# The orders of all five engine queues of a four-layer attention chain are rewritten, and its first five loads are dealt anew to two DMA-issuing queues

## Chip, cores and metric

One NeuronCore of a Trainium2 chip runs the kernel. The metric is the device time of one execution in microseconds (us), over three runs of the kernel before: 165.75, 165.82 and 166.11, median 165.82. A profiled execution of the same kernel is a run of its own and has its own time.

## What is computed

The input x is 8 images of 16 x 16 tokens with 128 channels, in float32. Four layers follow each other. Reduced to what matters (pieces of the reference; projections, biases and the second branch of layer 3 are left out):

```
# layer 0: attention with pooled keys and values
attn = softmax(theta(x) @ maxpool2x2(phi(x)).T)          # 256 x 64 an image
x = x + (attn @ maxpool2x2(g(x)) @ w_o + b_o) * sigma
# layer 1: group norm, attention with one head of 128 channels
x = x + softmax(q(gn(x)) @ k(gn(x)).T / sqrt(128)) @ v(gn(x)) @ wo + bo   # 256 x 256
# layer 2: group norm, attention with 8 heads of 16 channels
x = x + concat(softmax(q_h @ k_h.T / 4) @ v_h) @ w_out + b_out            # 8 x 256 x 256
# layer 3: Hartley transform over channels and width, block MLP, soft threshold, inverse
y = o2k + o2n
y = sign(y) * relu(abs(y) - 0.01)
x = x + dht2d(y) / (W * C)
```

Nothing passes from one image to another.

## The kernel before

The whole problem stays in the core's memory: the inputs are loaded once (x as tokens, `xin`; x with channels on the partitions, `x0T`; one table of weights, `tab`, in five column groups), and each image's result is stored once. All arithmetic is float32, for which each product on TensorE takes two passes, so a product shows as two MATMUL records.

Nothing schedules the work at run time. `build` holds five blocks, one for each engine queue: `sp` (SyncE, DMA issues alone), `pool` (GpSimd), `pe` (TensorE), `act` (ScalarE) and `dve` (VectorE). In each, small functions are defined that first wait for a semaphore of the step whose result they need and then issue that step for image i; behind them stands a list of calls, written out by hand, that is the order of that engine's queue. An engine works through its list strictly in that order. Extra pairs such as `("theta", 6)` in a call are added waits: on TensorE they hold a step until a PSUM bank's earlier content has been read, since the second argument of a TensorE call is the bank (0 to 7) that it writes.

The names used below, one call an image unless stated, with the line of the instruction in the profile:

- layer 0: `proj0` (TensorE L525), `pool0` (VectorE L1091), `pg_out` (GpSimd L407) and `phi_out` (L402), `theta` (ScalarE L870, two instructions), `s0` (TensorE L541), `nmax0_out` (VectorE L1097), `exp0` (ScalarE L888), `p0t` (TensorE L548, a transposition), `p0c` (ScalarE L895), `gwm` (TensorE L533), `gw` (ScalarE L881), `o0` (TensorE L556), `inv0_out` and `x1_out` (VectorE L1104, L1111), `x1b_out` (GpSimd L344);
- group norm before layers 1 and 2 (the second argument): `x1t`/`x2t` (TensorE L564/L628), `moments`, `mean` (VectorE L1121, L1126), `mean_square` (GpSimd L420), `gm1`/`gm2` (TensorE L571/L637), `variance`, `variance_eps` (VectorE L1133, L1139), `inverse_deviation` (GpSimd L359), `normalised` (VectorE L1148);
- layer 1: `qk1`, `v1m`, `s1` (TensorE L581, L590, L599), `q1`, `v1` (ScalarE L900, L907), `nmax1_out` (VectorE L1156), `score_shift` (GpSimd L429, two instructions), `exp1` (ScalarE L914), `p1t` (TensorE L609), `p1c` (ScalarE L921), `o1` (TensorE L619), `inv1_out`, `x2_out` (VectorE L1163, L1170), `x2b_out` (GpSimd L351);
- layer 2, heads in two sets g = 0 and 1: `qk2`, `v2m` (TensorE L647/L648, L655), `qkE`, `qkO`, `va` (ScalarE L928, L935, L941), `sm` (scores for the maxima, TensorE L671), `nmax2_out` (VectorE L1181, two halves a set), `nt` (TensorE L681), `nc_out` (ScalarE L948), `spread` (SyncE L287: a DMA of 8 KB that lays the maxima beside the queries), `st` (scores again, transposed and shifted, TensorE L692), `exp2` (ScalarE L954, two halves a set), `pv` (TensorE L703), `oc` (ScalarE L960), `ot` (TensorE L714), `oinv_out`, `on_out` (VectorE L1188, L1194), `ont` (TensorE L722), `onc` (ScalarE L965), `o2` (TensorE L730), `x3_out` (VectorE L1202);
- layer 3: `zm`, `am`, `ym`, `v3`, `om` (TensorE L744, L753/L755, L765/L766, L773, L782), `zc`, `odd_out`, `o1k_out`, `o1n_out`, `yh`, `s3_out` (ScalarE L970, L976, L982, L989, L998, L1003), `wrap`, `z_sum`, `z_difference` (GpSimd L365, L370, L413), `a_out`, `yn`, `xo` (VectorE L1211/L1212, L1219, L1227), `store` (SyncE L292).

Steps on weights alone (`fold_biases`, `fold_values`, `fold_biases2`, `fold_out2`, `fold_mlp` on TensorE; `scaled1`, `scaled2`, `bias_wide`, `bias_wide2`, `mlp_sums` on GpSimd; `values_scores`, `fold1_out` on ScalarE; `halves`, `mlp_folded` and others on VectorE) are strewn in among the first images. `keep_clock(n, b)` (TensorE L464) issues n bf16 products of zeros into bank b whose result nobody reads.

The five groups of the weight table are called tab0 (73.5 KB: the bias columns and `w0`, needed by the first product), tab1 (128 KB), tab2 (640 KB), tab3 (384 KB) and tab4 (708 KB). Two queues issue loads: SyncE and, for the first two of its own, ScalarE.

Of the kernel before, what the change touches and what calls it, by code (L numbers as in the profile page):

```python
# [126 lines left out]
def build(nc, x, xT, xT_rest, weights, out):  # L127


    with ExitStack() as ctx:  # L130
# [180 lines left out]
        def _(pool):  # L311
# [121 lines left out]
            pg_out(0); pg_out(1); phi_out(0); pg_out(2); phi_out(1); pg_out(3, ("gw_ps", 1), ("phi", 1)); phi_out(2)  # L433
            scaled1(0); phi_out(3, ("s0", 1)); scaled1(1); bias_wide(); scaled1(2); mean_square(0, 1); pg_out(4)
            scaled2(0); x1b_out(0); x1b_out(1); bias_wide2(); inverse_deviation(0, 1); mean_square(1, 1); x1b_out(2)
            scaled2(1); mlp_sums(); inverse_deviation(1, 1); mean_square(2, 1); score_shift(0); pg_out(5); x1b_out(3)
            pg_out(6); inverse_deviation(2, 1); scaled2(2); phi_out(4); phi_out(5); phi_out(6); pg_out(7, ("phi", 5))
            phi_out(7, ("s0", 5)); score_shift(1); x2b_out(0); mean_square(0, 2); mean_square(3, 1); score_shift(2)
            inverse_deviation(0, 2); x1b_out(4); mean_square(4, 1); inverse_deviation(3, 1); x2b_out(1); x2b_out(2)
            mean_square(1, 2); score_shift(3); mean_square(2, 2); inverse_deviation(1, 2); x1b_out(5)  # L440
            inverse_deviation(4, 1); inverse_deviation(2, 2); x1b_out(6); x2b_out(3); score_shift(4)
            mean_square(5, 1); mean_square(6, 1); mean_square(3, 2); inverse_deviation(5, 1); inverse_deviation(6, 1)
            x1b_out(7); inverse_deviation(3, 2); x2b_out(4); score_shift(5); score_shift(6); mean_square(4, 2)
            mean_square(7, 1); inverse_deviation(4, 2); inverse_deviation(7, 1); x2b_out(5); x2b_out(6); wrap(0)
            z_sum(0); z_difference(0); score_shift(7); mean_square(5, 2); mean_square(6, 2); x2b_out(7)
            inverse_deviation(5, 2); inverse_deviation(6, 2); wrap(1); mean_square(7, 2); z_difference(1); z_sum(1)
            inverse_deviation(7, 2); wrap(2); z_sum(2); z_difference(2); wrap(3); z_sum(3); z_difference(3); wrap(4)
# [4 lines left out]
        def _(pe):
# [339 lines left out]
            s0(3, 7, ("vo_rd", 1)); proj0(5, 6, ("gw", 4)); x1t(2, 0); proj0(6, 5, ("gw", 5))
            proj0(7, 2, ("b2_rd", 1)); fold_out2(3); qk1(0, 1); gm1(1); p0t(3, 3, ("o2_rd", 1)); v1m(0, 7); s1(0, 1)
            o0(3, 3); keep_clock(6, 6, ("theta", 6), ("v1", 1)); fold_mlp(6, 7); gm1(2); qk1(1, 3, ("x1", 4))
            gwm(5, 4); p1t(0, 1); s1(1, 3); v1m(1, 4, ("gw", 6)); s0(4, 1, ("p1T", 1))
            o1(0, 6, ("fold1_rd", 1), ("c_rd", 1)); qk1(2, 0); s0(5, 7); v1m(2, 2, ("theta", 8)); x1t(3, 4)
# [483 lines left out]
```

## Time and profile before

| | before |
|---|---|
| device time, three runs | 165.75, 165.82, 166.11 us (median 165.82) |
| profiled execution: its own time | 164.78 us |
| profiled execution: span of the core | 162.9 us |
| TensorE matmuls busy | 154.6 us |
| VectorE, ScalarE, GpSimd busy | 103.2, 107.1, 53.2 us |
| instructions | 3840 |

The span runs from the first to the last recorded instruction; the profiled execution's own time is 1.88 us longer and holds what lies around it, and the median of the unprofiled runs is 1.04 us above that time. TensorE's busy share is that of matmul records, which overlap their neighbours by a pipeline depth, so a busy TensorE may still be one that waits in small pieces.

### The profile page before, as it was taken

To read this page: it belongs to the slowest core of one execution; us is meant where nothing else is said; L and a number is where in the kernel's file an instruction comes from. 1 tells how busy PE (TensorE), PEld (TensorE's weight loads), DVE (VectorE), ACT (ScalarE), POOL (GpSimd) and SP (SyncE) were. 2 spreads that over 40 slices of the span, in tenths; PEclk is the share of its full clock that TensorE was granted. 3 is DMA by queue.
4 is the path that set the end of the run, shared out by engine and by line. 5 is a ranking of instruction groups with operands and counts; after the bars stand their busy time and mean duration, and the time that the engine had idled before them with its cause. 6 is when DMAs were issued, how large, how long until landed. Compare 5 with 4: busy or idle time off the path is not lost.

```text
span 162.9 us, 3840 instructions
## 1 busy us (share of the span) xinstructions
PE 154.6 (95%) x1461; PEld 118.7 (73%) x1461; DVE 103.2 (63%) x257; ACT 107.1 (66%) x245; POOL 53.2 (33%) x128
## 2 busy tenths in 40 slices
PE   5999999999999999999999999999999899999992
PEld 3899789877867677886576865777588576568892
DVE  0447977979789648665997664984397554015453
ACT  3577469854855685858366765838856768885770
POOL 6474988653722541530201153002002000016300
PEclk9999999999999999999999999999999999999999
DMA  5995000000000000000000000000001000100003
GB/s 146 252 395 209 0 6 4 0 4 0 0 0 8 0 0 4 4 0 6 0 4 4 4 32 4 0 10 0 0 4 36 32 8 4 36 0 0 0 4 129
DMA packets 3233, 5.50 MB, mean 34 GB/s; under 512 B 400, under 2 KB 2320, under 8 KB 3216
## 3 DMA queue, kind: packets, MB, share of 16 engines
q1 hardware_dynamic: 2928, 5.00, 9.1%
q8 instruction: 12, 0.20, 0.5%
q10 hardware_dynamic: 288, 0.26, 0.5%
q14 instruction: 5, 0.04, 0.1%
HBM read 4.08 MB, written 1.05 MB: 31 GB/s over the span
## 4 chain that ended last, share of the span: by engine, by line
PE 83%; ACT 5%; DVE 4%; POOL 2%; issue 2%; DMA 2%; SPq 0%; DVEq 0%; POOLq 0%
PE psum L692 9%; PE psum L703 9%; PE psum L671 9%; PE psum L619 5%; PE psum L599 5%; ACT pT L954 4%; PE psum L647 3%; PE psum L730 3%; PE psum L714 3%; PE psum L765 2%; PE psum L744 2%; PE psum L773 2%; PE psum L590 2%; DVE nmax L1181 2%; PE psum L609 2%; PE psum L766 2%
## 5 line engine op out<-in xcount | busy, mean ns | idle before, releaser
L1181 DVE TENSOR_REDUCE nmax<-psum 128x4 f32<-128x1024 f32 x32 | 38.1, 1218 | 10.2 <-PE psum L671 10.2
L954 ACT ACTIVATE pT<-psum 128x1024 f32<-128x1024 f32 x32 | 31.2, 1020 | 12.6 <-PE psum L692 12.6
L365 POOL COPY zE<-zE 128x17 f32<-128x17 f32 x8 | 1.6, 200 | 51.4 <-ACT zE L970 51.4
L692 PE MATMUL psum<-qk 32*128 32x256 f32 (+1 forms) x256 | 18.2, 399 | 0.1
L671 PE MATMUL psum<-qk 16*128 16x256 f32 (+1 forms) x256 | 18.1, 396 | 0.0
L703 PE MATMUL psum<-pT,vaug_all 128*32 128x256 f32 x256 | 17.1, 385 | 0.3 <-ACT pT L954 0.3
L692 PEld LDWEIGHTS psum<-qk 32*128 32x128 f32 (+1 forms) x256 | 11.6, 184 | 4.5 <-issue 1.8
L671 PEld LDWEIGHTS psum<-qk 16*128 16x128 f32 (+1 forms) x256 | 11.7, 184 | 4.0 <-DVE nmax L1181 1.2
L429 POOL TENSOR_SCALAR nb<-nmax,e 128x1 f32<-128x1 f32 x16 | 5.8, 372 | 19.3 <-DVE nmax L1156 11.1
L703 PEld LDWEIGHTS psum<-pT,vaug_all 128*32 128x32 f32 x256 | 6.8, 109 | 6.4 <-issue 2.5
L1148 DVE TENSOR_SCALAR xn<-psum,rstd 128x256 f32<-128x256 f32 x16 | 8.5, 540 | 2.6 <-POOL rstd L359 2.6
L359 POOL TENSOR_TENSOR rstd<-vare,half 128x1 f32<-128x1 f32 x16 | 8.7, 555 | 3.3 <-DVE vare L1139 3.1
L619 PEld LDWEIGHTS psum<-v_all,p1T 128*128 128x128 f32 x64 | 7.8, 191 | 1.6 <-issue 1.6
L351 POOL TENSOR_TENSOR x0T<-x,b_out 128x256 f32<-128x256 f32 x8 | 5.8, 728 | 9.4 <-DVE x L1170 9.4
L619 PE MATMUL psum<-v_all,p1T 128*128 128x129 f32 x64 | 8.9, 281 | 0.0
L599 PE MATMUL psum<-xn,t1T 128*128 128x256 f32 x32 | 8.6, 392 | 0.0
L914 ACT ACTIVATE p<-psum,nb 128x256 f32<-128x256 f32 x16 | 6.7, 473 | 2.9 <-POOL nb L429 2.7
L960 ACT COPY oT<-psum 128x256 f32<-128x256 f32 x16 | 5.9, 371 | 3.8 <-PE psum L703 3.6
L420 POOL TENSOR_SCALAR mv<-mv 128x1 f32<-128x1 f32 x16 | 5.4, 343 | 9.1 <-DVE mv L1126 9.0
L464 PE MATMUL psum<-busy 128*128 128x256 bf16 x35 | 6.7, 313 | 1.4 <-DVE busy L1030 1.0
L870 ACT ACTIVATE theta_all<-psum,tab 32x128 f32<-32x128 f32 x16 | 5.8, 362 | 3.3 <-DVE pooled L1091 2.9
L928 ACT ACTIVATE qk<-psum,q_bias 128x512 f32<-128x512 f32 x8 | 5.5, 690 | 2.8 <-PE psum L648 2.7
(163 smaller groups left out, 354.7 us busy)
## 6 DMA issues: line engine op xcount, KB each, us to landing
out<-x SPq DMA_DIRECT2D x8, 128.0 KB, 1.9
tab<-in_weights SPq DMA_DIRECT2D x1, 708.0 KB, 9.4
tab<-in_weights SPq DMA_DIRECT2D x1, 640.0 KB, 4.8
xin<-in_x SPq DMA_DIRECT2D x2, 256.0 KB, 6.8
x0T<-in_xT_rest SPq DMA_DIRECT2D x1, 512.0 KB, 7.1
xin<-in_x SPq DMA_DIRECT2D x1, 512.0 KB, 8.1
x0T<-in_xT SPq DMA_DIRECT2D x3, 128.0 KB, 3.2
tab<-in_weights SPq DMA_DIRECT2D x1, 384.0 KB, 8.4
```

Of the source, the lines that this page charges most:

```text
L359: gp.tensor_tensor(rstd[k](i), vare[k](i), half[:, :], ALU.pow).then_inc(s[f"rstd{layer}"], 1)
L464: mm(bank[b][:, 0:256], busy[:, 0:P], busy[:, :], start=True, stop=True)
L599: last = mm(bank[b][:, u * TOK:(u + 1) * TOK], t1T(i)[:, u * P:(u + 1) * P], xn[0](i), start=True, stop=True)
L619: last = mm(bank[b][:, u * (C + 1):(u + 1) * (C + 1)], p1T(i)[:, m, u * P:(u + 1) * P], v1_all[:, i % SLOTS, m, :], start=(m == 0), stop=( ...
L671: last = mm(bank[(b0, b1)[j // 2] + j % 2][:, u * TOK:(u + 1) * TOK], at[:, u, 0, :], at[:, :, 1, :], start=True, stop=True)
L692: last = mm(bank[(b0, b1)[j // 2] + j % 2][:, m * TOK:(m + 1) * TOK], at[:, m, 1, :], at[:, :, 0, :], start=True, stop=True)
L703: last = mm(bank[b][32 * j:32 * j + 32, 0:TOK], vaug_all[:, i % SLOTS, m, QUADS * g + j, :], pT[g](i)[:, j, m, :], start=(m == 0), stop=(m ...
L914: last = go(p1(i)[:, u, :], bank[home["s1", i]][:, u * TOK:(u + 1) * TOK], ACT.Exp, bias=nb1(i)[:, u:u + 1])
L954: go(pT[g](i)[:, 2 * k:2 * k + 2].rearrange("p j m t -> p j (m t)"), pair(home["st", g, i][k]), ACT.Exp).then_inc(s["exp" + "EO"[g]], 1)
L960: copy(oT[g](i), bank[home["pv", g, i]][:, 0:TOK]).then_inc(s["oT" + "EO"[g]], 1)
L1148: v.tensor_scalar(xn[k](i), x[:, 0:TOK], x[:, TOK:TOK + 1], rstd[k](i), ALU.subtract, ALU.mult).then_inc(s[f"xn{layer}"], 1)
L1181: v.tensor_reduce(nmax2(i)[:, g, 2 * k:2 * k + 2, :], pair(home["sm", g, i][k]).rearrange("p j (u m) -> p j u m", u=TILES), AX.X, ALU.max, ...
```

## The change

No step is added or taken away except for the products of zeros: 35 before, 31 now. What changes is the order of the calls in the lists of all five blocks, the PSUM banks and added waits of the TensorE calls that go with it, and who issues which of the first loads. ScalarE's queue issued x0T of image 1 and tab1, and now issues tab0 and tab1. SyncE's issued x0T of image 0, tab0, x0T of images 2 and 3, and now issues x0T of images 0, 1, 2 and 3. The core of the diff, of the order lists only their beginnings or the pieces that are spoken of:

```diff
-            load_x(sp.dma_start, 0)
-            load_table(sp.dma_start, 0)
-            load_x(sp.dma_start, 2)
-            load_x(sp.dma_start, 3)
+            load_x(0)
+            load_x(1)
+            load_x(2)
+            load_x(3)
             load_table(sp.dma_start, 2)
...
-            spread(3, 1); store(0); spread(4, 1); spread(4, 0); spread(5, 0); spread(5, 1); store(1); store(2)
-            spread(6, 0); spread(6, 1); spread(7, 0); spread(7, 1); store(3); store(4); store(5); store(6); store(7)
+            spread(3, 1); spread(4, 1); spread(4, 0); spread(5, 0); store(0); spread(6, 0); spread(5, 1); store(1)
+            spread(6, 1); spread(7, 0); spread(7, 1); store(2); store(3); store(4); store(5); store(6); store(7)
...
-            keep_clock(9, 7); proj0(0, 0); proj0(1, 1); proj0(2, 2); keep_clock(1, 7); proj0(3, 3)
-            gwm(0, 0, ("theta", 1)); gwm(1, 4); s0(0, 5); keep_clock(2, 7); gwm(2, 1, ("theta", 2)); keep_clock(2, 7)
+            keep_clock(11, 7); proj0(0, 0); proj0(1, 1); keep_clock(4, 7); proj0(2, 2); proj0(3, 0, ("theta", 1))
+            s0(0, 1, ("theta", 2)); gwm(0, 3); gwm(1, 4); gwm(2, 5); s0(1, 2, ("theta", 3)); s0(2, 6)
...
-            am(5, 3); zm(7, 2); am(6, 6); ym(4, 7); keep_clock(3, 5); am(7, 6, ("aneg", 7)); ym(5, 3); ym(6, 2)
+            am(6, 0); ym(4, 1); om(3, 2, ("z", 8)); am(7, 3, ("aneg", 6)); ym(5, 0, ("aneg", 7)); v3(4, 1)
...
-            load_x(nc.scalar.dma_start, 1)
+            load_table(nc.scalar.dma_start, 0)
             load_table(nc.scalar.dma_start, 1)
...
-            theta(0); theta(1); theta(2); exp0(0); gw(0); p0c(0); exp0(1); gw(1); p0c(1); gw(2); exp0(2); theta(3)
-            p0c(2); values_scores(); theta(4); gw(3); gw(4); exp0(3); q1(0); p0c(3); v1(0); theta(5); exp1(0)
+            theta(0); theta(1); theta(2); exp0(0); gw(0); p0c(0); exp0(1); exp0(2); gw(1); values_scores(); p0c(1)
+            theta(3); theta(4); p0c(2); gw(2); theta(5); theta(6, ("s0", 4)); q1(0); gw(3); v1(0); gw(4); exp1(0)
```

`load_x` is now a local function of SyncE's block that issues on that queue.

Three places show how instructions move. GpSimd, at the group norm of image 0 before layer 1 (L420 is `mean_square`, L407 `pg_out`, L389 `scaled2`, L344 `x1b_out`, L394 `bias_wide2`, L359 `inverse_deviation`); before:

```order
L420 TENSOR_SCALAR mv<-mv 128x1
L407 TENSOR_TENSOR pg<-pooled,tab 128x128
L389 TENSOR_SCALAR w2n<-tab 128x128
L344 TENSOR_TENSOR xin<-x,bo_wide 128x256 x2
L394 COPY bv_wide<-bv 128x128
L359 TENSOR_TENSOR rstd<-vare,half 128x1
```

and in the change, where L402 is `phi_out` and L334/L336 are `mlp_sums`:

```order
L420 TENSOR_SCALAR mv<-mv 128x1
L407 TENSOR_TENSOR pg<-pooled,tab 128x128
L359 TENSOR_TENSOR rstd<-vare,half 128x1
L402 TENSOR_TENSOR phi_all<-pg,tab 128x128
L407 TENSOR_TENSOR pg<-pooled,tab 128x128 x2
L389 TENSOR_SCALAR w2n<-tab 128x128
L334 TENSOR_TENSOR mlp_a<-mlp_half 128x256
```

The inverse deviation of image 0 has moved ahead of four GpSimd instructions that stood between it and `pg_out`; the two `x1b_out` now come behind `mlp_sums` and the last `scaled2`.

TensorE, from there to the first product of layer 1 (L581 is `qk1` of image 0, L571 the first `gm1`); before:

```order
L564 MATMUL psum<-tab,x 128x128 x2
L556 MATMUL psum<-gw_all,p0T 128x258
L571 MATMUL psum<-mv,tab 128x2
L496 MATMUL psum<-tab 128x1
L497 MATMUL psum<-tab 128x1
L533 MATMUL psum<-w0s,pg 128x128
L541 MATMUL psum<-phi_all,theta_all 128x128
L525 MATMUL psum<-x0T,tab 128x256
L564 MATMUL psum<-tab,x 128x128 x2
L525 MATMUL psum<-x0T,tab 128x256 x2
L503 MATMUL psum<-tab,bv_wide 128x128
L581 MATMUL psum<-xn,w1qk 128x256
```

and in the change:

```order
L525 MATMUL psum<-x0T,tab 128x256 x3
L571 MATMUL psum<-mv,tab 128x2
L548 MATMUL psum<-tab,p 128x128
L556 MATMUL psum<-gw_all,p0T 128x258
L541 MATMUL psum<-phi_all,theta_all 128x128
L464 MATMUL psum<-busy 128x256 x5
L496 MATMUL psum<-tab 128x1
L497 MATMUL psum<-tab 128x1
L533 MATMUL psum<-w0s,pg 128x128
L556 MATMUL psum<-gw_all,p0T 128x258
L581 MATMUL psum<-xn,w1qk 128x256
```

Ahead of `qk1` of image 0 there were `x1t` of images 1 and 2, `proj0` of image 7, `gwm` of image 4 and `fold_out2`; all five now come behind it, and five products of zeros stand in the stretch.

TensorE, from the last transposed scores (L692, `st(7, 1)`) to `ot` of image 7 (L714, the last one); before:

```order
L692 MATMUL psum<-qk 128x256 x8
L714 MATMUL psum<-tab,oT 128x128 x4
L744 MATMUL psum<-tab,x 128x136 x2
L722 MATMUL psum<-tab,on 128x128 x2
L703 MATMUL psum<-pT,vaug_all 32x256 x8
L722 MATMUL psum<-tab,on 128x128 x2
L703 MATMUL psum<-pT,vaug_all 32x256 x8
L730 MATMUL psum<-tab,onT 128x128 x4
L714 MATMUL psum<-tab,oT 128x128 x4
```

and in the change:

```order
L692 MATMUL psum<-qk 128x256 x8
L703 MATMUL psum<-pT,vaug_all 32x256 x8
L722 MATMUL psum<-tab,on 128x128 x2
L744 MATMUL psum<-tab,x 128x136 x2
L714 MATMUL psum<-tab,oT 128x128 x4
L703 MATMUL psum<-pT,vaug_all 32x256 x8
L730 MATMUL psum<-tab,onT 128x128 x2
L722 MATMUL psum<-tab,on 128x128 x2
L714 MATMUL psum<-tab,oT 128x128 x4
```

One of two `o2` has gone behind the last `ot`; so has, from further ahead than these rows, `om` of image 3, which now stands between `ym(4)` and `am(7)` in the place where three products of zeros stood.

## Rows read from the trace of the kernel before

**Rows 1.** The profile page: busy time of the engines, and the chain that ended last by engine

```profile
PE 154.6 (95%) x1461; PEld 118.7 (73%) x1461; DVE 103.2 (63%) x257; ACT 107.1 (66%) x245; POOL 53.2 (33%) x128
...
PE 83%; ACT 5%; DVE 4%; POOL 2%; issue 2%; DMA 2%; SPq 0%; DVEq 0%; POOLq 0%
```

**Rows 2.** Windows: stretch, its length, busy us (instructions) of each engine, TensorE clock, DMA share, GB/s

```profile
110.00:120.00 10.00, 9.71 (x98) 6.96 (x98) 5.16 (x9) 8.86 (x16) 1.14 (x3) 1.00 0.01 2
```

**Rows 3.** Timeline of the opening: start, us, engine, line, operation, count, idle before

```profile
0.72 0.39 SPq L258 DMA_DIRECT2D x0T<-in_xT  x1
...
1.04 2.10 PE L464 MATMUL psum<-busy 128*128 128x256 bf16 x9 [1.04 <-DVE busy L1030]
...
1.17 0.41 SPq L254 DMA_DIRECT2D tab<-in_weights  x1
...
3.97 2.93 PE L525 MATMUL psum<-x0T,tab 128*128 128x256 f32 x6 [0.83 <-DMA tab<-in_weights]
...
7.79 0.39 PE L541 MATMUL psum<-phi_all,theta_all 128*128 128x128 f32 x2
```

**Rows 4.** DMA issues: queue, count, KB of one, us from issue to landing

```profile
x0T<-in_xT SPq DMA_DIRECT2D x3, 128.0 KB, 3.2
...
x0T<-in_xT ACTq DMA_DIRECT2D x1, 128.0 KB, 3.0
...
tab<-in_weights SPq DMA_DIRECT2D x1, 73.5 KB, 2.8
```

**Rows 5.** The chain that ended last, 7 to 19 us: start, us, what

```profile
7.07 0.43 PE psum L525 x2
...
15.53 1.38 POOL xin L344 x2
...
17.10 0.57 POOL rstd L359
...
17.70 0.56 DVE xn L1148
...
18.39 0.67 PE psum L581 x2
```

**Rows 6.** Timeline, 12 to 24 us

```profile
14.72 0.74 ACT L870 ACTIVATE theta_all<-psum,tab 32x128 f32<-32x128 f32 x2 [0.29 <-DVE pooled L1091]
14.75 0.28 PE L571 MATMUL psum<-mv,tab 128*128 128x2 f32 x2
...
20.79 0.69 DVE L1156 TENSOR_REDUCE nmax<-psum 128x2 f32<-128x512 f32 x1 [0.48 <-PE psum L599]
...
21.59 0.73 POOL L429 TENSOR_SCALAR nb<-nmax,e 128x1 f32<-128x1 f32 x2
...
22.34 0.84 ACT L914 ACTIVATE p<-psum,nb 128x256 f32<-128x256 f32 x2 [1.22 <-POOL nb L429]
...
23.84 0.60 PE L609 MATMUL psum<-tab,p 128*128 128x128 f32 x4
```

**Rows 7.** The chain that ended last: first products of layer 2, and one later wait

```profile
33.29 0.43 PE psum L647 x2
...
35.18 1.12 PE psum L671 x16
...
140.20 1.03 ACT pT L954
```

**Rows 8.** The chain that ended last, from the last `st` on

```profile
141.28 1.15 PE psum L692 x16
...
147.16 0.44 PE psum L714 x4
...
160.03 0.42 DVE x L1227
```

**Rows 9.** Timeline: the first `nt` and the first `st`, which waits for a `spread`

```profile
49.69 0.27 PE L681 MATMUL psum<-tab,nmax 128*16 128x128 f32 x1
...
52.45 0.92 PE L692 MATMUL psum<-qk 32*128 32x256 f32 x11
```

More of the change, by code:

```diff
@@ L432, in _ @@
             fill()
[L433 to L447, printed above, removed]
@@ L792, in _ @@
[L792 to L796, printed above, removed]
@@ new lines, in _ @@
+            x2t(0, 2, ("v1", 2)); s1(2, 6); gwm(5, 0, ("x1", 4)); s0(6, 1); x1t(3, 5, ("v1", 3)); p1t(1, 7); gm2(0)
+            o0(4, 3, ("p0", 6)); o1(1, 7); p1t(2, 6); gm1(3); x1t(4, 1, ("p0", 7)); qk2(0, 4); o1(2, 0, ("gw", 6))
+            sm(0, 0, 6, 2, ("x2", 2)); qk1(3, 4, ("qkO", 1)); x2t(1, 0, ("x2", 3)); v1m(3, 5); s1(3, 4)
+            s0(7, 5, ("v1", 4)); gwm(6, 6, ("nmaxE", 1)); gwm(7, 7); p0t(5, 2, ("nmaxE", 2)); x2t(2, 3); o0(5, 2)
+            v2m(0, 7, ("gw", 8)); gm1(4); keep_clock(1, 6); gm2(1); gm2(2); p1t(3, 2, ("x1", 6))
@@ new lines, in _ @@
+            sm(0, 1, 6, 4, ("vaug", 1)); o1(3, 2); p0t(6, 0, ("xn2", 2)); qk2(1, 1); o0(6, 0); qk1(4, 6, ("nmaxO", 1))
+            qk2(2, 3); v1m(4, 1, ("qkO", 2)); sm(1, 1, 6, 4, ("q1", 5), ("nmaxO", 2)); nt(0, 1, ("v1", 5))
+            s1(4, 2, ("x2", 4)); v2m(1, 1, ("stage", 1)); v2m(2, 0, ("x1", 7)); x1t(5, 3, ("qkO", 3))
+            keep_clock(2, 0, ("vaug", 3), ("vaug", 2), ("nmaxO", 3)); st(0, 1, 0, 6); x2t(3, 4, ("nmaxO", 4))
+            p1t(4, 2); gm1(5); x1t(6, 5); gm2(3); o1(4, 2); st(0, 0, 6, 0, ("expO", 2)); qk1(5, 3)
@@ new lines, in _ @@
+            v1m(5, 2, ("x2", 5)); gm1(6); pv(0, 1, 4, ("xn2", 4)); sm(1, 0, 0, 6, ("expE", 2)); s1(5, 3)
+            qk1(6, 2, ("v1", 6)); pv(0, 0, 0, ("nmaxE", 3)); p0t(7, 2, ("q1", 7)); s1(6, 1); o0(7, 2)
+            v1m(6, 0, ("oTE", 1)); x2t(4, 6, ("nmaxE", 4)); p1t(5, 3); qk2(3, 2, ("x1", 8)); x1t(7, 3, ("p1T", 6))
+            nt(1, 0); ot(0, 7); o1(5, 5); v2m(3, 0, ("stage", 2)); gm1(7); gm2(4); p1t(6, 7, ("on", 1))
+            ont(0, 2, ("qkO", 4)); st(1, 0, 0, 4, ("vaug", 4), ("x2", 6)); o1(6, 2, ("onT", 1)); o2(0, 3, ("xn1", 8))
@@ L1009, in _ @@
-            gw(7); exp1(3); va(0); p1c(3); exp0(7); qkE(1); qkO(1); va(1); qkE(2); q1(4); qkO(2); nc_out(0); v1(4)
-            va(2); p0c(7); exp1(4); exp2(0, 1, 0); exp2(0, 1, 1); p1c(4); oc(0, 1); exp2(0, 0, 0); exp2(0, 0, 1)
-            q1(5); qkE(3); q1(6); qkO(3); v1(5); v1(6); exp1(5); oc(0, 0); nc_out(1); exp1(6); p1c(5); va(3); onc(0)
-            p1c(6); exp2(1, 0, 0); exp2(1, 0, 1); exp2(1, 1, 0); exp2(1, 1, 1); qkE(4); q1(7); qkO(4); zc(0); oc(1, 0)
-            nc_out(2); odd_out(0); o1k_out(0); oc(1, 1); o1n_out(0); v1(7); va(4); yh(0); exp2(2, 1, 0); exp2(2, 1, 1)
@@ new lines, in _ @@
+            exp0(7); exp1(3); va(0); p1c(3); p0c(6); qkE(1); qkO(1); q1(4); v1(4); qkE(2); nc_out(0); qkO(2); va(1)
+            va(2); exp1(4); exp2(0, 1, 0); p1c(4); exp2(0, 1, 1); exp2(0, 0, 0); exp2(0, 0, 1); q1(5); oc(0, 1); v1(5)
+            q1(6); p0c(7); oc(0, 0); exp1(5); v1(6); p1c(5); qkE(3); nc_out(1); exp1(6); qkO(3); va(3); p1c(6); onc(0)
+            exp2(1, 0, 0); exp2(1, 0, 1); exp2(1, 1, 0); exp2(1, 1, 1); qkE(4); zc(0); qkO(4); v1(7); oc(1, 1)
+            odd_out(0); nc_out(2); o1k_out(0); o1n_out(0); q1(7); oc(1, 0); va(4); yh(0); exp2(2, 1, 0); exp2(2, 1, 1)
```

191 lines of the change are left out of this document (99 added, 92 removed).

## The prediction

> **What bounds the kernel now.** I read the page first. TensorE's matmul records cover 95% of the span and 83% of the chain that ended last runs through them; ScalarE, VectorE and GpSimd hold 5, 4 and 2% of it [rows 1]. So the order on TensorE is the schedule, and two things can move the time: less waiting between its steps, or the same waiting filled with work needed anyway. Since the busy share counts a matmul that sits in a pipeline, I made a ledger instead: each call's price is what it takes on the chain when nothing holds it, such as 0.43 us for a product of 256 columns [rows 5], 1.07 for one set of `sm` or `st` [rows 7] (1.12 there with its hand-over), 0.44 for an `ot` [rows 8]. All useful calls come to some 136.3 us in both versions, the 35 products of zeros to 3.9 (0.11 each) and now 3.4. Of the 162.9 us, then, TensorE spends 26.6 without useful work. Where that lies is read as start time minus useful work ahead of the call in the list:
>
> - `p1t(0)`, 23.84 us [rows 6], 14.2 ahead: 9.7 lost already.
> - `sm(0, 0)`, 35.11 (35.18 less its hand-over) [rows 7], 24.1 ahead: 11.0 lost.
> - the last `st`, 141.28 [rows 8], 119.6 ahead: 21.7 lost.
> - `ot(7)`, 147.0 (147.16 less the same), 124.9 ahead: 22.1. The rest is the end.
>
> The first 24 us lose as much as the 106 behind `sm(0, 0)`. They are a chain of small steps over four engines and not yet a full TensorE.
>
> **The opening, loads.** tab0 was issued second on SyncE at 1.17 and lands 2.8 later, when the first product starts at 3.97 [rows 3, 4]. Issued first on ScalarE, at the time of SyncE's first (0.72) it would land near 3.5. Then x0T of image 0 (also 0.72, and 3.0 to 3.2 to land, rows for other images [rows 4]) decides, near 3.7: 0.27 sooner. x0T of image 1 is issued 0.45 later, lands by 4.4, and is needed after the first product, at 4.6: covered. If that cover fails it costs what it is late, under 0.3.
>
> The Trainium skill, page "DMA: Bandwidth & Descriptors", section "Issuing engines are not separate DMA queues", says that transfers of all issuers share the same 16 engines and that a second issuer saves only issue time. By it tab0 and x0T of image 0, now issued at once, slow each other and this 0.27 is nothing; by the rows it is 0.27. The sum below needs it only for its own size.
>
> **The opening, chain of image 0.** The first six passes took 0.49 each (2.93 over 6), against 0.22 for one soon after (0.43 over 2) [rows 3, 5], at a granted clock of full speed in the page: the first behave as at 1.2 GHz, the others as at 2.4. I price `proj0` of images 0 and 1 and the four zeros behind them at the slow rate: 0.86, 0.86 and 0.85. `proj0(2)` then starts at 6.3, no sooner than now. But `s0(0)` has only `theta(1)` to wait for, done near 7.0, and starts at 7.1 instead of 7.79 [rows 3]. `theta(2)` (0.74 [rows 6]) holds `exp0(0)` to 8.2, so `o0(0)` gains 0.45, not 0.7.
>
> Then the reordered GpSimd list. Before, `gm1(0)` ran at 14.75 [rows 6], and its `inverse_deviation` began at 17.10, after two `x1b_out` of 1.38 together; xn of image 0 began at 17.70 and `qk1(0)` at 18.39 [rows 5]. In the change, `fold_values` starts at 10.4 (three `scaled1` and `bias_wide` end near 10.2) and takes 1.1, `x1t(0)` 0.22, zeros 0.22, three `proj0` 1.3: `gm1(0)` at 13.3. VectorE finishes a `pool0` and has the variance by 14.1; GpSimd is free, rstd takes 0.57 to 14.7, xn 0.56 to 15.3. `qk1(0)` does not start then: its mark wants `theta(5)`, and ScalarE has `values_scores`, three `theta` pairs (2.2), two `p0c` and a `gw` to do, which I add up to 15.7. I take 15.85: 2.5 sooner, with 1.3 us less useful work done. Net, 1.2.
>
> From there: `s1(0)` at 17.0, maxima done at 18.8 (0.69), `score_shift` 0.73, `exp1` 0.84 [rows 6]: `p1t(0)` at 20.4 instead of 23.84, with 1.5 less work ahead: net 1.9 us. What is late next is GpSimd, which has put off three `x1b_out` (2.1 us, at half of 1.38 each) until just before `score_shift(1)`; I get it done at 27.1, when `exp1(1)` can start.
>
> Both orders have exactly the same calls ahead of `sm(0, 0)`, so its start compares directly. Followed through in the same way: `x2t(0)` 26.4, `p1t(1)` 28.1, `exp1(2)` 29.45 to 30.3, `p1t(2)` to 30.8, its copy to 31.65, `gw(5)` to 32.2, `qk2(0)` 31.3 instead of 33.12 (33.29 less its hand-over [rows 7]), `qkE(0)` to 33.1. `sm(0, 0)` starts at 33.2 instead of 35.11: **minus 1.9 us**. My chain leaves out some hand-overs of 0.03 to 0.14, the gaps between the chain's pieces [rows 5]; on a dozen in a row that is up to 1.0, so the bounds are -0.9 and -2.4, the latter with the slow clock ended before `proj0(2)`.
>
> **The middle, `sm(0, 0)` to the last `st`.** Nothing is added; the sets ahead of `st(1, 0)` and `st(2, 1)` are again the same in both. The loss there, 10.7 us over 106, is in pieces under a microsecond, such as the one where `st` of a set waits for the 1.03 of an `exp2` [rows 7]. I followed four places of the new order (first `st`, `spread` of image 5, `nt(6)`, `st(5, 0)`) and found neither a wait of over 0.3 us that is new nor one that is gone. I take **0**. The nearest row for a bound either way is that one `exp2`: 1.03, gained or lost once.
>
> **The end.** `om(3)` (0.44) and one `o2` (0.44) have gone behind `ot(7)`, so the chain from `ot(7)` to the last `xo` starts 0.9 sooner. That chain now ends at 160.45 (160.03 + 0.42) and takes 13.45 [rows 8]. With the new order I get 13.7: `om(3)` takes the place of zeros, and the last `ym` wait for ScalarE's `o1k_out` and `o1n_out` either way. **Minus 0.6**, bounds 0 (the chain grows by all that is moved into it) and -0.9.
>
> **Sum.** -1.9 + 0 - 0.6 = -2.5. The profiled execution would have a span of 160.4 and a time of 162.3; against the median of the runs, 165.82, the forecast is **163.3 us**. Bounds of the terms together: +0.1 (-0.9 + 1.0 + 0) and -4.3 (-2.4 - 1.0 - 0.9), which can't all fall together; for the forecast's own case 162.3 to 164.5.
>
> **Rivals.**
>
> 1. The lead is given back in the middle. For it: in one stretch ScalarE is busy 8.86 of 10 us [rows 2], so there its 32 `exp2` of 1.03 may set the pace, and a TensorE that comes earlier waits longer. Against: over the span ScalarE has 107.1 us of work to TensorE's 154.6 [rows 1], and every engine had the same lead at `sm(0, 0)`. It would leave the end and a fifth of the rest, 0.6 + 0.4: 164.8. Chance 0.18.
>
> 2. The clock. Before, TensorE ran zeros for 2.10 us, stood still for 0.83 and then ran six passes at the slow rate [rows 3]. Eleven zeros leave a gap of some 0.2, so full speed may come while the four zeros run, and `proj0(2)` 0.5 sooner: 162.8. Chance 0.06. The Trainium skill, page "TensorE: Matmul & The Clock Gate", Part 1, says that sustained activity releases the throttle and that the point of release varies between runs. By it this rival is somewhat likelier than I make it, or the gain differs from run to run.
>
> 3. Slower: SyncE's queue. `spread(5, 1)` now stands behind `spread(6, 0)`, which waits for `nc_out(6)`, and `nt(6)` comes 5.1 us of work earlier than it did, right behind four `nmax2_out` in a row. From `nt` to the `st` that needs the row is at most 2.76 us [rows 9], some 3.4 with a second issue in between; TensorE has 4.1 of work there. It starts to cost when `nt(6)`'s copy is 0.7 late, and the whole comes out slower when it is late by 0.7 + 2.5 + 0.3 = 3.5, for instance if VectorE comes to those four that late. A 4.5 delay gives 165.82 - 2.5 + 3.8 = 167.1. Against: VectorE is busy only 5.16 of 10 us just ahead of that place [rows 2]. Chance 0.10.
>
> 4. No change: opening and middle cancel, as when my missed hand-overs are a microsecond and one `exp2` is lost besides: about 165.8. Chance 0.06.
>
> **How the numbers follow.** The forecast has 0.60. About 0.2% (0.33 us) is what a measurement of this kernel can tell from no change. Faster: 0.60, 0.06 and nearly all of rival 1 (0.16) make 0.82. Same: rival 4 and what is left of rival 1, 0.08. Slower: 0.10. The range must reach from the lower edge of the case to rival 1 with some spread: 162.2 to 165.6.
>
> **What would show it.** `s0(0)` near 7.1; `gm1(0)` near 13.3 and `qk1(0)` near 15.9; `p1t(0)` near 20.4 and `sm(0, 0)` near 33.2; the last `st` some 2.3 sooner than 141.28, which is 1.9 and the 0.44 of `om(3)` moved behind it; 13.7 from `ot(7)` to the end of the last `xo`. If `sm(0, 0)` is on time and the last `st` is not, rival 1 holds; if `st(5, 1)` stands behind a DMA, rival 3. If `qk1(0)` is later than 17.4, my reading of the opening was wrong.

## The result

| | before | changed kernel |
|---|---|---|
| device time, median (range) | 165.86 us (165.75 to 166.11, 6 runs) | 162.95 us (162.55 to 163.25, 6 runs) |
| profiled execution: its own time | 164.78 us | 162.82 us |
| profiled execution: span | 162.9 us | 160.9 us |

The ratio is 0.9822 with a 95% interval of 0.9806 to 0.9838: 2.9 us faster, where 2.5 were forecast. A later comparison on another chip gave 0.9853 (0.9827 to 0.9878). The profiled executions differ by less, 1.96 us. That difference is itself a finding; it comes back below.

The page of the changed kernel, busy time and chain (against [rows 1]):

```profile
PE 154.1 (96%) x1457; PEld 118.4 (74%) x1457; DVE 102.4 (64%) x257; ACT 106.7 (66%) x245; POOL 53.0 (33%) x128
...
PE 85%; DMA 4%; ACT 3%; DVE 2%; POOL 2%; issue 1%; SPq 1%; DVEq 0%
```

TensorE has nearly the same work in a shorter span. On the chain, ScalarE and VectorE fell from 9% to 5%, and loads rose from 2% to 4%. The same stretch as [rows 2]:

```profile
110.00:120.00 10.00, 10.00 (x111) 6.76 (x110) 6.98 (x11) 7.38 (x16) 1.13 (x3) 1.00 0.01 2
```

The opening, timeline of the changed kernel (against [rows 3] and [rows 6]; in these views L872 is `theta`, L916 `exp1`, L1158 `nmax1_out`):

```profile
0.72 0.89 ACTq L254 DMA_DIRECT2D tab<-in_weights  x2
...
1.04 2.53 PE L464 MATMUL psum<-busy 128*128 128x256 bf16 x11 [1.04 <-DVE busy L1032]
3.39 1.87 PE L525 MATMUL psum<-x0T,tab 128*128 128x256 f32 x4
5.10 0.60 PE L464 MATMUL psum<-busy 128*128 128x256 bf16 x4
5.54 1.12 PE L525 MATMUL psum<-x0T,tab 128*128 128x256 f32 x4
6.72 0.49 PE L541 MATMUL psum<-phi_all,theta_all 128*128 128x128 f32 x2
...
8.49 1.29 POOL L377 TENSOR_TENSOR w1n<-tab 128x128 f32<-128x128 f32 x3 [0.73 <-DMA tab<-in_weights]
...
13.49 0.28 PE L571 MATMUL psum<-mv,tab 128*128 128x2 f32 x2
...
14.44 0.56 POOL L359 TENSOR_TENSOR rstd<-vare,half 128x1 f32<-128x1 f32 x1 [0.56 <-DVE vare L1141]
...
14.91 1.50 ACT L872 ACTIVATE theta_all<-psum,tab 32x128 f32<-32x128 f32 x4
...
15.04 0.55 DVE L1150 TENSOR_SCALAR xn<-psum,rstd 128x256 f32<-128x256 f32 x1 [0.33 <-POOL rstd L359]
...
15.74 0.60 PE L556 MATMUL psum<-gw_all,p0T 128*128 128x258 f32 x2
16.18 0.59 PE L581 MATMUL psum<-xn,w1qk 128*128 128x256 f32 x2
...
20.96 0.66 PE L609 MATMUL psum<-tab,p 128*128 128x128 f32 x4 [0.17 <-ACT p L916]
```

The zeros now run straight into the first product, and nothing stands between `gm1(0)` at 13.49 and its rstd but VectorE's variance. The chain that ended last, its end (against [rows 8]):

```profile
139.49 1.07 PE psum L692 x16
140.57 1.00 PE psum L703 x16
...
144.74 0.44 PE psum L714 x4
...
158.07 0.42 DVE x L1229
```

The starts of the milestones, from the timelines of both profiled executions, and what each stretch gained:

| | before | changed | gained since the row above |
|---|---|---|---|
| `sm(0, 0)` | 35.11 | 34.06 | 1.05 |
| `st(1, 0)` | 69.70 | 68.13 | 0.52 |
| last `st` | 141.28 | 139.42 | 0.29 (0.44 is `om(3)`, moved away) |
| `ot(7)` | 147.00 | 144.58 | 0.56 (0.44 is `o2(6)`, moved away) |
| end of the last `xo` | 160.45 | 158.49 | -0.46 |

They add up to 1.96 us. The first two rows of the table, before and then changed:

```profile
35.11 1.15 PE L671 MATMUL psum<-qk 16*128 16x256 f32 x16
...
69.70 1.15 PE L692 MATMUL psum<-qk 17*128 17x256 f32 x16
```

```profile
34.06 1.15 PE L671 MATMUL psum<-qk 16*128 16x256 f32 x16
...
68.13 1.15 PE L692 MATMUL psum<-qk 17*128 17x256 f32 x16
```

### The profile page after: what moved, and what is told of

Same layout as the page of the kernel before. It is cut to its first block, busy times and chain, and to the rows that moved or that the text cites. A ratio compares the mean times of both kernels' runs of the same rounds, so it can differ in the third digit from the quotient of the medians.

```text
span 160.9 us, 3845 instructions
## 1 busy us (share of the span) xinstructions
PE 154.1 (96%) x1457; PEld 118.4 (74%) x1457; DVE 102.4 (64%) x257; ACT 106.7 (66%) x245; POOL 53.0 (33%) x128
## 3 DMA queue, kind: packets, MB, share of 16 engines
HBM read 4.08 MB, written 1.05 MB: 32 GB/s over the span
## 4 chain that ended last, share of the span: by engine, by line
PE 85%; DMA 4%; ACT 3%; DVE 2%; POOL 2%; issue 1%; SPq 1%; DVEq 0%
PE psum L692 11%; PE psum L703 10%; PE psum L671 9%; PE psum L619 5%; PE psum L599 5%; DMA tab<-in_weights 4%; PE psum L744 3%; PE psum L730 3%; PE psum L773 3%; PE psum L647 3%; PE psum L714 2%; PE psum L581 2%; PE psum L655 2%; PE psum L590 2%; PE psum L765 2%; PE psum L766 2%
## 5 line engine op out<-in xcount | busy, mean ns | idle before, releaser
L956 ACT ACTIVATE pT<-psum 128x1024 f32<-128x1024 f32 x32 | 31.7, 1022 | 9.4 <-PE psum L692 9.4
L692 PE MATMUL psum<-qk 32*128 32x256 f32 (+1 forms) x256 | 18.3, 400 | 0.0
L692 PEld LDWEIGHTS psum<-qk 32*128 32x128 f32 (+1 forms) x256 | 11.6, 184 | 3.7 <-DVE nmax L1183 1.1
L359 POOL TENSOR_TENSOR rstd<-vare,half 128x1 f32<-128x1 f32 x16 | 8.8, 558 | 8.2 <-DVE vare L1141 8.2
L420 POOL TENSOR_SCALAR mv<-mv 128x1 f32<-128x1 f32 x16 | 5.5, 345 | 17.5 <-DVE mv L1128 17.5
L916 ACT ACTIVATE p<-psum,nb 128x256 f32<-128x256 f32 x16 | 6.7, 473 | 2.2 <-POOL nb L429 2.2
L1123 DVE BATCH_NORM_STATS2 bn<-psum 128x6 f32<-128x256 f32 x16 | 6.7, 423 | 2.3 <-PE psum L564 1.3
L1190 DVE RECIPROCAL oinv<-psum 128x16 f32<-128x16 f32 x8 | 2.0, 253 | 8.8 <-PE psum L714 8.7
L464 PE MATMUL psum<-busy 128*128 128x256 bf16 x31 | 6.2, 325 | 1.3 <-DVE busy L1032 1.0
L872 ACT ACTIVATE theta_all<-psum,tab 32x128 f32<-32x128 f32 x16 | 5.8, 362 | 2.5 <-DVE pooled L1093 2.2
```

The lines of the kernel that those rows point to most:

```text
L359: gp.tensor_tensor(rstd[k](i), vare[k](i), half[:, :], ALU.pow).then_inc(s[f"rstd{layer}"], 1)
L464: mm(bank[b][:, 0:256], busy[:, 0:P], busy[:, :], start=True, stop=True)
L692: last = mm(bank[(b0, b1)[j // 2] + j % 2][:, m * TOK:(m + 1) * TOK], at[:, m, 1, :], at[:, :, 0, :], start=True, stop=True)
L916: last = go(p1(i)[:, u, :], bank[home["s1", i]][:, u * TOK:(u + 1) * TOK], ACT.Exp, bias=nb1(i)[:, u:u + 1])
L956: go(pT[g](i)[:, 2 * k:2 * k + 2].rearrange("p j m t -> p j (m t)"), pair(home["st", g, i][k]), ACT.Exp).then_inc(s["exp" + "EO"[g]], 1)
L1123: v.bn_stats(bn[layer - 1](i), bank[home[f"x{layer}t", i]][:, 0:TOK]).then_inc(s[f"bn{layer}"], 1)
```

## The experiments

Twelve runs in three batches, each batch with the kernel before on the same chip (165.39, 165.45 and 165.49 us median, each over 20 to 28 runs). Where an experiment is judged by its profiled execution, the distance between two milestones is used, because a late opening carries through as a constant.

### The halves

**Before once more.**

> The kernel before, unchanged, profiled again. Its first profiled execution took 164.78 us, 1.0 below the lowest of its unprofiled runs (165.75), while that of the changed kernel (162.82) lies inside its own (162.55 to 163.25). Theory A, the first profile was a fortunate execution: this one spans about 163.9 us, and the microsecond shows in one stretch, most likely the opening, where sm(0,0) starts near 36 instead of 35.11. Theory B, the profiler always shortens this kernel: the span is 162.9 again and sm(0,0) starts at 35.1. Ratio 1.000 within 0.002.

Measured 165.46 us (164.68 to 166.40), ratio 1.0007 (0.9979 to 1.0035). The profiled execution was the fastest of the twelve runs, span 162.9 us and `sm(0, 0)` at 35.09, as theory B has it. But the profiler does not always shorten: later kernels were profiled at their median (12 zeros, 164.40 us against 164.41) or above it (the end alone, 165.74 against 165.68). The range of 1.7 us, from the same program, is the first thing to explain.

**Front only.** The changed kernel's orders, loads and zeros up to `sm(0, 0)` on all engines but SyncE's own list, the orders of before behind it.

```
-            keep_clock(9, 7); proj0(0, 0); proj0(1, 1); proj0(2, 2); ...
+            keep_clock(11, 7); proj0(0, 0); proj0(1, 1); keep_clock(4, 7); proj0(2, 2); ...
...
-            sm(0, 0, 6, 2, ("x2", 2)); qk1(3, 4, ("qkO", 1)); ...
+            sm(0, 0, 2, 6, ("x2", 2), ("xn2", 1), ("x1", 5), ("p1T", 3)); x2t(1, 5, ("qkO", 1), ("xn1", 4))
```

The first two lines are against the kernel before, the last two against the changed kernel, at the seam, where banks of two orders meet and some waits are added.

> The changed kernel's orders, loads and zeros up to sm(0,0) and its neighbours in time on the other engines, the kernel before's orders behind that. Theory A, the opening carries the gain (my forecast, -1.9 of -2.5): 163.8 to 164.3 us. Theory B, the opening brings what the two profiles show at sm(0,0), -1.05, and a middle that was ordered for another opening gives part of it back: 164.8 to 165.3.

Measured 164.17 us (163.79 to 164.44), ratio 0.9923 (0.9893 to 0.9952). `sm(0, 0)` starts at 34.34 instead of 35.11, and from there to the last `xo` it takes 0.19 more than before, behind the seam of two orders that were not made for each other. The time lies in theory A's range, but its premise does not hold: the opening brought 0.77 in the profile, not 1.9. The 1.2 of the median is more than the profile shows, as with the whole change.

**Back only.** The mirror image: before up to `sm(0, 0)`, the changed orders behind it.

```
-            gm1(3); ...; qk2(0, 5); o1(2, 0); sm(0, 0, 2, 6, ("x2", 2))
+            sm(0, 0, 6, 2, ("x2", 2), ("p0", 7), ("v1", 3)); qk1(3, 4, ("qkO", 1), ("xn1", 4)); x2t(1, 0, ("x2", 3))
```

Here too some waits are added at the seam.

> The kernel before up to sm(0,0), the changed kernel's orders behind it. Theory A, middle 0 and end -0.6: 165.2 us. Theory B, what the two profiles show behind sm(0,0), -0.95: 164.9. If the two parts only pay together, 165.8 or more.

Measured 164.39 us (164.08 to 164.98), ratio 0.9938 (0.9917 to 0.9958). From `sm(0, 0)` to the start of the last three `xo` it takes 123.13 us; before takes 124.03 and the changed kernel 123.12. So the back is worth 0.9 us with either front ahead of it, near theory B's 0.95 (the median fell by 1.0; both theories' times were reckoned from 165.82, where this batch has 165.39), and the front does not give its lead away in the middle: rival 1 is out.

### The loads, and what a wait before the first product costs

**Loads only.** In the kernel before, tab0 on ScalarE's queue first, x0T of image 1 on SyncE's.

```
-            load_table(sp.dma_start, 0)
+            load_x(sp.dma_start, 1)
...
-            load_x(nc.scalar.dma_start, 1)
+            load_table(nc.scalar.dma_start, 0)
```

> The kernel before with the changed kernel's first five loads alone (tab0 on ScalarE's queue, x0T of image 1 on SyncE's). The first product starts at 3.4 to 3.7 instead of 3.97. Theory A, the chain of the opening is tight: -0.3 to -0.6, 165.3 to 165.5 us. Theory B, it is absorbed by the next wait (theta, GpSimd): 165.7 to 165.9.

Measured 164.35 us (163.72 to 164.79), ratio 0.9928 (0.9902 to 0.9954). Neither theory had that. The first product starts at 3.41 us, yet the profiled span is 0.1 us shorter and no more. The median fell by 1.0. One profiled execution would have called this edit worthless; the runs put it at a third of the whole gain. What changed ahead of the first product, besides its start, is TensorE's idle time: 0.27 us instead of 0.83. Hence a third theory, named C in the next expectations: idle time there puts off TensorE's full speed, in most executions.

**Before with 12 zeros**, which fill the wait and change no load.

```
-            keep_clock(9, 7); proj0(0, 0)
+            keep_clock(12, 7); proj0(0, 0)
```

> The kernel before with 12 products of zeros at the start instead of 9, which fills TensorE's wait of 0.6 to 0.8 us for the first load. Theory C: the spread of the kernel before (164.7 to 166.4) is the point at which TensorE comes to its full speed, and an idle stretch before the first product makes it late in most executions: median 164.4 to 164.9, spread under 1.1, while the profiled span hardly moves. Theory D: the spread has nothing to do with that wait: median and spread as before, 165.4.

Measured 164.41 us (163.83 to 164.82), ratio 0.9932 (0.9908 to 0.9956): three products of zeros are worth as much as the loads, and theory C holds. The timeline:

```profile
1.04 2.74 PE L464 MATMUL psum<-busy 128*128 128x256 bf16 x12 [1.04 <-DVE busy L1030]
3.84 2.74 PE L525 MATMUL psum<-x0T,tab 128*128 128x256 f32 x6
```

**Changed loads with 6 zeros**: early loads, but the wait open again.

```
-            keep_clock(9, 7); proj0(0, 0)
+            keep_clock(6, 7); proj0(0, 0)
```

> The kernel before with the changed loads (164.35 us when run alone) and 6 products of zeros instead of 9, so that TensorE waits some 0.9 us again although the load is early. Theory C: the median goes back to 165.1 to 165.5 and the spread to over 1.4 us. Theory D: the loads gained as loads, 164.3 to 164.6.

Measured 165.21 us (164.26 to 166.04), ratio 0.9987 (0.9959 to 1.0016). The gain is gone, and the range is 1.8 us wide again, although the first product comes at 3.51. That is theory C. (This kernel has both a longer wait and three zeros fewer; that the wait counts by itself is told by the loads-only kernel, which kept its 9 zeros.)

```profile
1.04 1.46 PE L464 MATMUL psum<-busy 128*128 128x256 bf16 x6 [1.04 <-DVE busy L1030]
3.51 3.12 PE L525 MATMUL psum<-x0T,tab 128*128 128x256 f32 x6 [1.00 <-DMA tab<-in_weights]
```

**The changed kernel with the old loads.**

```
-            load_x(1)
+            load_table(sp.dma_start, 0)
...
-            load_table(nc.scalar.dma_start, 0)
+            nc.scalar.dma_start(x0T(1), xT[1]).then_inc(s["x0T1"], 16)
```

> The changed kernel with the loads of the kernel before (x0T of image 1 on ScalarE's queue, tab0 second on SyncE's). Its 11 zeros leave a wait of only 0.2 to 0.4. Theory C: only the later load counts, +0.3 to +0.5 over the changed kernel. Theory D: it loses what the loads alone gained, 1.0.

Measured 163.22 us (162.72 to 163.73), ratio 0.9869 (0.9842 to 0.9896). Its 11 zeros leave 0.21 us open, and it is 0.3 to 0.4 slower than the changed kernel in the other two batches by the medians, 0.3 to 0.8 by the ratios to the kernel before. Theory C holds better than D, but no changed kernel ran on this chip, so the size is rough.

**The changed kernel again, and with 13 zeros**, on one chip.

```
-            keep_clock(11, 7); proj0(0, 0)
+            keep_clock(13, 7); proj0(0, 0)
```

> The changed kernel once more, on the same chip as these runs: the yardstick for the run with 13 zeros. All theories: median 162.6 to 163.2, ratio 0.980 to 0.986, the profiled execution between 162.4 and 163.6 according to where full speed comes.

> Edit to the changed kernel: 13 products of zeros at the start instead of 11. Theory C (what costs is idle time between the zeros and the first product, which puts full speed off in most executions): the changed kernel's zeros end only 0.0 to 0.2 ahead of its loads in the profiled execution, but later loads in others can reopen the gap; two more zeros keep it shut and cost at most 0.46 at the slow rate where the loads are early; the median is between 0.3 below and 0.2 above that of the changed kernel of the same batch. Theory D (a slower start is a slower start): the first product 0.3 to 0.46 later, and the median as much above.

Measured 162.83 us (162.75 to 163.18), ratio 0.9853 (0.9827 to 0.9878), and 163.32 us (162.80 to 163.57), ratio 0.9873 (0.9849 to 0.9897). Thirteen are 0.5 us worse, outside what theory C allowed and near theory D: with nothing left to fill, the zeros only push the first product back, here from 3.46 to 3.79 us. These are six runs against five, and the two intervals overlap.

```profile
1.04 2.96 PE L464 MATMUL psum<-busy 128*128 128x256 bf16 x13 [1.04 <-DVE busy L1032]
3.79 1.60 PE L525 MATMUL psum<-x0T,tab 128*128 128x256 f32 x4
...
7.10 0.67 PE L525 MATMUL psum<-x0T,tab 128*128 128x256 f32 x2 [0.85 <-DMA x0T<-in_xT]
```

In this execution x0T of image 3 was late as well, so its profile, 0.6 us behind at `sm(0, 0)`, holds two things. No version that I ran beats the changed kernel.

### Single moves out of the GpSimd list

**The inverse deviation alone moved ahead.**

```
-            scaled2(0); x1b_out(0); x1b_out(1); bias_wide2(); inverse_deviation(0, 1); mean_square(1, 1)
+            inverse_deviation(0, 1); scaled2(0); x1b_out(0); x1b_out(1); bias_wide2(); mean_square(1, 1)
```

> The kernel before with one call moved: GpSimd's inverse_deviation of image 0 goes in front of scaled2(0), two x1b_out and bias_wide2. rstd is then ready near 16.9 instead of 17.7. Theory A: this was the wait that set qk1(0), and qk1(0) starts 0.5 to 0.8 sooner, behind which sm(0,0) and the whole follow by 0.3 or more: 164.7 to 165.1. Theory B: TensorE has work to do there in any case (it ran until 18.07), qk1(0) comes 0.3 sooner at most, and the delayed x1b_out and bias_wide2 take it back: 165.3 to 165.6.

Measured 167.49 us (166.35 to 168.09), ratio 1.0129 (1.0093 to 1.0164): 2 us slower, which neither theory had. (Its profiled execution had a late opening as well, `gm1(0)` at 16.22 instead of 14.75. From `gm1(0)` to the end of the span it takes 149.5 us, 1.3 more than before; the other 0.7 of the median, over six runs, is not placed.) The timeline names what took the place of the wait removed:

```profile
20.55 0.49 PE L503 MATMUL psum<-tab,bv_wide 128*128 128x128 f32 x2 [1.23 <-POOL bv_wide L394]
20.87 0.60 PE L581 MATMUL psum<-xn,w1qk 128*128 128x256 f32 x2
```

`fold_out2` stands ahead of `qk1(0)` in TensorE's list, and its operand `bias_wide2` now waits behind both `x1b_out`.

**The copy and the inverse deviation moved ahead together.**

```
-            scaled2(0); x1b_out(0); x1b_out(1); bias_wide2(); inverse_deviation(0, 1); mean_square(1, 1)
+            bias_wide2(); inverse_deviation(0, 1); scaled2(0); x1b_out(0); x1b_out(1); mean_square(1, 1)
```

> Edit to the kernel before: on GpSimd bias_wide2 and inverse_deviation(0, 1) stand ahead of scaled2(0) and of the two x1b_out; nothing else moves. The run with the call of inverse_deviation alone came out 2 us slower, because fold_out2 on TensorE, which stands ahead of qk1(0), then waited for bias_wide2. Theory F (that wait is the whole reason): with the copy in front as well, inverse_deviation(0, 1) starts 1.74 us behind gm1(0) instead of 2.35, fold_out2 waits for nothing, qk1(0) starts 3.1 to 3.3 behind gm1(0) (before: 3.64), and the lead of 0.3 to 0.5 is kept to sm(0, 0); the span is 162.4 to 162.7 if the opening is as before, and the median 0.2 to 0.5 below that of before. Theory G (x1b_out is what matters: done 1 us later, it holds x2_out and layer 1's end): qk1(0) comes sooner but sm(0, 0) not; span and median as before or above.

Measured 166.08 us (165.28 to 167.09), ratio 1.0057 (1.0031 to 1.0082). Theory F's first half came true, `qk1(0)` 3.16 us behind `gm1(0)` instead of 3.64; then the lead was lost one step later:

```profile
17.74 0.64 PE L581 MATMUL psum<-xn,w1qk 128*128 128x256 f32 x2
19.27 0.38 PE L571 MATMUL psum<-mv,tab 128*128 128x2 f32 x2 [0.89 <-POOL mv L420]
...
24.32 0.60 PE L609 MATMUL psum<-tab,p 128*128 128x128 f32 x4
```

`gm1(1)` follows `qk1(0)` and needs `mean_square(1, 1)`, which stands behind the two `x1b_out` as well. `sm(0, 0)` is 0.48 later than in the profile of before, though the opening was 0.17 sooner. So theory F falls, and theory G's outcome came by another path: the late `x1b_out` does matter, but it costs at `gm1(1)` and has its full price at `p1t(0)` already (0.48 later), ahead of any `x2_out`. From `gm1(0)` to the end of the span the profile takes 0.7 us more than before, as the median has it (0.6). What the change moves on GpSimd pays only with TensorE's list rewritten beside it (in the change `fold_out2` and `gm1(1)` come 3.8 and 4.2 us behind `qk1(0)`).

### The end alone

The kernel before with `om(3)` and `o2(6)` behind `ot(7)` and the changed orders from the last `st` on.

```
-            ot(5, 0, ("stage", 8)); om(3, 1); pv(6, 1, 6)
+            ot(5, 0, ("stage", 8)); pv(6, 1, 6)
...
-            st(7, 1, 0, 2, ("expE", 15)); ot(6, 6); ...
+            st(7, 1, 6, 2, ("expE", 15), ("on", 6), ("oTE", 7), ("expO", 14)); pv(7, 0, 1, ("oTE", 7), ("expE", 15)); ...
```

> Edit to the kernel before: om(3) and o2(6) stand behind ot(7), xo(3) late, and everything from the last st on is in the changed kernel's order on TensorE, ScalarE and VectorE. Theory A (the end's share of the gain is the work moved behind ot(7), less what the chain grows by): last st 0.44 sooner than 141.28, ot(7) 0.9 sooner than 147.0, 13.9 from there to the last xo instead of 13.45, so the last xo 0.4 sooner and the span 162.5; the median 0.2 to 0.6 below that of before. Theory B (the end gained only together with the changed middle, where the exponentials of image 7 come sooner): the last st comes 0.44 sooner, but the exponentials of image 7 hold ot(7), which starts 0.0 to 0.4 sooner; the span is 162.9 or above.

Measured 165.68 us (165.03 to 166.21), ratio 1.0006 (0.9982 to 1.0029). From `sm(0, 0)` the profile has 106.22 us to the last `st` (before: 106.17) and 111.37 to `ot(7)` (before: 111.89). The last `st` did not come 0.44 sooner; it waits (here L691 is `st`, L954 `exp2`, L960 `oc`):

```profile
140.63 1.07 PE L702 MATMUL psum<-pT,vaug_all 128*32 128x256 f32 x16
142.35 1.15 PE L691 MATMUL psum<-qk 32*128 32x256 f32 x16 [0.65 <-ACT pT L954]
...
140.77 1.02 ACT L954 ACTIVATE pT<-psum 128x1024 f32<-128x1024 f32 x1 [0.46 <-PE psum L691]
141.77 0.37 ACT L960 COPY oT<-psum 128x256 f32<-128x256 f32 x1
```

It starts 0.2 us after that `oc` ended. This spliced kernel puts the last `st` into bank 6, whose earlier content is copied only behind the exponential; before, in bank 0, it wanted the exponential alone. So theory A falls, and so does theory B's first half; the splice has a wait of its own, and the run does not tell what the end alone is worth. What it does show, as the back-only run does: from `ot(7)` to the last three `xo` the changed order takes 12.60 us against 12.14, 0.46 us more for the 0.88 that was moved in.

## Why the prediction was right

**The sign and the size** came out: 162.95 us measured, 163.3 forecast. Two of the three terms, however, were off, and an effect that the sum left at nothing made up for them. That the size came out within 0.4 us is in part luck: the profiled spans fell by 1.96, where 2.5 were forecast, and a constant 1.04 between profile and median would have made that 163.9.

- **Loads.** The first product started at 3.39 us, 0.58 sooner than in the profile of before, where the row gave 0.27. Of the 0.58, up to 0.2 is the late load of that one profile: with the old loads the other first products came at 3.78 to 3.98. And x0T of image 0, which I expected to decide near 3.7, landed 2.4 us after its issue, not 3.0 to 3.2, so that tab0 decided. The start was right in kind; what I had wrong was the price. It is not the 0.3 us of the earlier start but the closed wait: 1.0 us of the median as the only edit, some 0.3 on top of 11 zeros. The Trainium skill, page "DMA: Bandwidth & Descriptors", section "Issuing engines are not separate DMA queues", would have had the small table gain nothing but issue time. The traces show just such a gain, issue 0.45 us sooner, and no slowing that would eat it up: tab0 took 2.6 to 2.8 us to land in all fourteen profiles, at the side of x0T and behind it. For the large table the same holds: tab2, needed by `w1n`, took 5.8 us in the changed kernel's profile against 4.8 before, and GpSimd waited 0.73 for it; but over all profiles it took 4.6 to 6.3 with the new loads and 4.8 to 6.3 with the old ones.
- **The opening, forecast -1.9, measured -1.05** in the profiles. Its steps held in order: `s0(0)` 6.72 (7.1 forecast), `gm1(0)` 13.49 (13.3), `qk1(0)` 16.18 (15.85), `p1t(0)` 20.96 (20.4), `sm(0, 0)` 34.06 (33.2). The reordered GpSimd list did what I read in it: rstd at 14.44 instead of 17.10 [rows 5]. The step that failed is the reading behind it. The mark of `theta(5)` was no hold, since ScalarE had it at 15.66; TensorE came to `qk1(0)` straight from its own `o0`. The 0.38 by which `s0(0)` came sooner than forecast was gone at `fold_values`, which waited for GpSimd's `bq_wide` and started at 10.39 (10.4 forecast). From there each piece of the chain up to `p1t(1)` added 0.1 to 0.2 that I had left out: `x2t(0)` at 27.10 for 26.4, `p1t(1)` at 28.91 for 28.1. The total, 0.86, lies inside the 1.0 that I had set aside as a bound, and should have been in the sum.
- **The middle, forecast 0, measured -0.37** (0.52 gained to `st(1, 0)`, 0.15 lost from there to the last `st`, `om(3)` not counted). No wait appeared at the four places that I had followed, and the result lies inside the bound of one `exp2`. Part of it is seen: the `exp2` of [rows 7] held the last `st` 0.2 us beyond the `pv` before it, and in the changed kernel that `st` follows its `pv` at once. Where the 0.52 ahead of `st(1, 0)` lay stays open: TensorE's recorded idle time in that stretch is the same, 1.08 us before and 1.05 in the change, and one product of zeros fewer makes 0.11.
- **The end, forecast -0.6, measured -0.54** with the 0.44 of `om(3)`: ahead of `ot(7)` it took out 1.00 (0.44 for `om(3)`; 0.56 for `o2(6)` and a small wait), and the chain from there takes 13.91 instead of 13.45, where I had 13.7. About half of the 0.88 moved behind `ot(7)` lengthened the chain; I had it at a quarter.
- **Rival 2, the clock**, had a chance of 0.06 and was partly what happened. In the changed kernel's profile the four zeros take 0.44 us from their start to the next product's, which is 0.11 each, so full speed is there at 5.1 us; before, it is there at 6.9, where two passes of 256 columns take 0.43 [rows 5] (a start of 7.07 in that view). The clock records of the two traces have it from 4.93 and from 6.90 us. Since `fold_values` waited for GpSimd all the same, this lead is not part of the 1.05 at `sm(0, 0)` one for one. The terms add up to 1.96 us between the two profiles, and the median fell by 2.9. The rest is that the runs of the kernel before lay 1.1 us above its profiled execution (165.86 to 164.78), and those of the changed kernel 0.1 above its own (162.95 to 162.82); I had carried the 1.04 over as a constant. It was not one. An execution of the kernel before that reaches full speed late fits the first number, as the section on the hardware shows; the unprofiled runs themselves have no record of it.
- **Rival 3, SyncE's queue**, did not come: `st(5, 1)` started at 125.53 and waited for nothing. **Rival 1** fell with the two halves.

By the medians, the back alone is worth 1.0 us and the front alone, with its loads and zeros, 1.2 with 0.2 lost at the seam; the whole is worth 2.7 to 2.9, so 0.3 to 0.5 shows in neither half. The closed wait is 1.0 where it is the only edit, and some 0.3 on top of the new zeros. How the front's gain splits between its order and its zeros was not measured apart.

## What to carry to other kernels

When one engine carries the chain, move a step on a helper engine only together with everything that the main engine's list wants from that helper nearby: single moves out of this order cost 0.6 and 2 us of the median. Fill the wait before the first product with warm-up work that ends when the loads land, neither before nor after. And judge an edit to the opening by several runs, since one profiled execution showed 0.1 us of an effect of 1.0.
